# Layer 3 of a four-layer stack: the Walsh-Hadamard transform split between VectorE butterflies and the gate and up weights

## The reference, cut to what matters

```python
def _L3_ffn_ref(input, SU_ug, SU_dp, Wscale_ug, Wscale_dp, W_up, W_gate, W_down):
    HIDDEN = 512
    INTER = 2048
    SCALE = 64.0

    def fwht(x):
        orig_shape = x.shape
        n = orig_shape[-1]
        x = x.reshape(-1, n)
        h = 1
        while h < n:
            x = x.reshape(-1, n // (2 * h), 2, h)
            a, b = (x[:, :, 0, :], x[:, :, 1, :])
            x = jnp.stack([a + b, a - b], axis=2).reshape(-1, n)
            h *= 2
        return (x / jnp.sqrt(jnp.asarray(n, x.dtype))).reshape(orig_shape)
    n = SU_ug.shape[0]
    x = input.reshape(-1, n)
    x = fwht(x * SU_ug) / SCALE
    x_up = x @ W_up.T * (Wscale_ug[:INTER] * SCALE)
    x_gate = x @ W_gate.T * (Wscale_ug[INTER:] * SCALE)
    x = jax.nn.silu(x_gate) * x_up
    x = fwht(x * SU_dp) / SCALE
    x = x @ W_down.T * (Wscale_dp * SCALE)
    return x.reshape(input.shape)
```

## Time and profile before

| | us |
|---|---|
| median of 3 runs | 1707.26 (1704.78 to 1709.21) |
| the profiled execution | 1706.87 |
| its span, first to last instruction | 1705.1 |

### The profile page before, as it was taken

One profiled execution on the slowest core, in us unless ns is written; L12 is line 12 of the kernel. 1 busy time (PEld: TensorE's weight loads), 2 busy tenths in 40 slices (PEclk: granted clock), 3 DMA queues, 4 the chain that ended last, 5 costly groups with the idle time before them and its releaser, 6 DMA issues.

```text
span 1705.1 us, 19577 instructions
## 1 busy us (share of the span) xinstructions
PE 1506.5 (88%) x6453; PEld 970.9 (57%) x6486; DVE 1118.1 (66%) x1718; ACT 969.6 (57%) x1270; POOL 453.4 (27%) x418
## 2 busy tenths in 40 slices
PE   5676579999975899996599999699999999999997
PEld 2222234444432566665544444378788888888886
DVE  6899589999996999995767777754322222222222
ACT  5766499999985889985267868544321221221211
POOL 0000133544421111110144544540231331331311
PEclk9999799999998999998599999899999999999999
DMA  7766642221216877765653545660110110100001
GB/s 279 273 205 208 238 149 64 73 71 62 69 37 178 232 187 182 184 145 206 235 163 136 183 151 170 202 226 1 37 38 1 38 37 1 37 31 8 1 22 77
DMA packets 102998, 206.16 MB, mean 121 GB/s; under 512 B 11061, under 2 KB 27957, under 8 KB 99189
## 3 DMA queue, kind: packets, MB, share of 16 engines
q1 hardware_dynamic: 90308, 173.72, 29.8%
q0 software_dynamic: 12592, 31.20, 8.2%
HBM read 140.13 MB, written 52.17 MB: 113 GB/s over the span
## 4 chain that ended last, share of the span: by engine, by line
PE 49%; DVE 2%; DMA 1%; ACT 1%; issue 0%; POOL 0%; SPq 0%; DVEq 0%; POOLq 0%; ACTq 0%
PE ffn_po L2532 10%; PE ffn_pg L2513 10%; PE ffn_pu L2513 10%; PE moe_psum L1920 8%; PE moe_psum L1941 4%; PE ffn_po L1614 2%; PE ffn_po L1601 2%; PE moe_psum L1859 1%; PE moe_psum L1908 1%; DVE x L2602 1%; PE moe_psum L1931 0%; DMA in_part<-expert_out,moe_source 0%; DVE x L1647 0%; DVE rt_hot_block L2213 0%; DMA rt_consts<-in_route 0%
## 5 line engine op out<-in xcount | busy, mean ns | idle before, releaser
L2435 ACT ACTIVATE up_front<-ffn_pg,ffn_gate_chunk 128x512 f32<-128x512 f32 x64 | 44.1, 689 | 320.7 <-PE ffn_pg L2513 271.7
L2592 DVE SCALAR_TENSOR_TENSOR up_front<-ffn_pu,ffn_up_scale,up_front 128x512 f32<-128x512 f32 x64 | 48.0, 750 | 231.6 <-PE ffn_pu L2513 231.5
L2486 POOL TENSOR_TENSOR ffn_hl<-up_front,ffn_hh 128x512 fp32r<-128x512 f32 x64 | 82.8, 1295 | 396.4 <-ACT ffn_hh L2442 396.4
L2602 DVE SCALAR_TENSOR_TENSOR x<-ffn_po,ffn_out_scale,x 128x512 f32<-128x512 f32 x128 | 87.2, 744 | 146.8 <-PE ffn_po L2532 146.8
L2532 PE MATMUL ffn_po<-ffn_hh,ffn_wh 128*128 128x512 f32 x256 | 100.7, 393 | 4.2 <-DVE x L2602 2.9
L2513 PE MATMUL ffn_pg<-zhi,ffn_wh 128*128 128x512 f32 x256 | 101.5, 396 | 0.5
L2513 PE MATMUL ffn_pu<-zhi,ffn_wh 128*128 128x512 f32 x256 | 100.8, 394 | 0.0
L2513 PE MATMUL ffn_pg<-zhi,ffn_wl 128*128 128x512 f32 x256 | 100.4, 392 | 0.0
L2513 PE MATMUL ffn_pu<-zhi,ffn_wl 128*128 128x512 f32 x256 | 100.4, 392 | 0.0
L2532 PE MATMUL ffn_po<-ffn_hh,ffn_wl 128*128 128x512 f32 x256 | 100.1, 391 | 0.0
L2513 PE MATMUL ffn_pg<-zlo,ffn_wh 128*128 128x512 f32 x256 | 99.6, 389 | 0.0
(11 more groups left out here) (353 smaller groups left out, 4076.5 us busy)
## 6 DMA issues: line engine op xcount, KB each, us to landing
wkv_k<-in_fside SPq DMA_DIRECT2D x64, 256.0 KB, 4.4
ratio<-wkv_fn SPq DMA_DIRECT2D x64, 256.0 KB, 2.4
wkv_ek<-exp_k SPq DMA_DIRECT2D x48, 256.0 KB, 3.0
wkv_ekv<-exp_k_times_v SPq DMA_DIRECT2D x48, 256.0 KB, 3.5
expert_out<-moe_eo SPq DMA_DIRECT2D x39, 256.0 KB, 2.1
up_front<-in_gated SPq DMA_DIRECT2D x8, 1024.0 KB, 5.1
x<-in_x SPq DMA_DIRECT2D x4, 1024.0 KB, 6.8
down_first_a<-in_down_raw SPq DMA_DIRECT2D x16, 256.0 KB, 2.7
```

The lines of the kernel that those rows point to most:

```text
L2435: eng.activation(hf[t], p_g[t][:, :], ACT.Silu, scale=scale).then_inc(*E(f"silu{t}").inc)
L2486: eng.tensor_tensor(hl[t][slot % 2][:, :], hf[t], hh[t][slot % 2][:, :].bitcast(F32), ALU.subtract).then_inc(*E(f"hl{t}").inc)
L2592: eng.scalar_tensor_tensor(hf[t], p_u[t][:, :], scale, hf[t], ALU.mult, ALU.mult).then_inc(*E(f"h{t}").inc)
L2602: last = eng.scalar_tensor_tensor(x[:, o, :], p_o[:, o, :], out_s[:, o:o + 1], x[:, o, :], ALU.mult, ALU.add)
```

## The change

The transform of z is taken apart. Its part over the four channel tiles is done on DVE with butterflies, in float32, before z is split into high and low: `inner` (two pairs, a sum and a difference each) and `outer` (the same across the pairs), eight 128x512 additions or subtractions for each unit. They use the four tiles of z and one spare tile, which is the memory of the first four diagonal matrices. After that z_high and z_low are made once, in the order AS_MADE in which the outer results appear; the second rounding (`round_transformed`, `low_transformed`) is gone, and so is `fwht` with its 32 matmuls for each unit.

The part inside a tile (H128) is symmetric and moves to the weights. `turn_weights(m)` multiplies the gate and up weights of chunk m with H128: 2048 columns in four pieces of 512, two matmuls (high, low) each, into the four banks of gate and up; `high_turned` (ACT) and `low_turned` (DVE) bring each piece back over the old weights as a high and a low part. That is done once for each of the 8 chunks: for the first before the first `cols_of_y`, for the second after down(2), for the others after down(i - 1) at i % 4 = 2 (i = 6, 10, ..., 26). On DVE `low_turned` stands behind `add(i - 1)`. The next step's products wait each for its own piece, so that its bank is free; after i = 3 the first product waits for all four pieces.

The order of the input stage is a new one: gate_up(0) as a whole after cols_of_y(1), then a product of gate, cols_of_y(2), and so on. `gate` of a new unit waits for all of z_low of the unit before, and diagonals(i + 1) stand behind z_low(i) as before.

```diff
+AS_MADE = (2, 0, 3, 1)
...
-        self.minus_H = sb("in3_minus_H", [P, P], F32R)
-        self.diag = [[sb(f"in3_diag{k}_{t}", [P, P]) for t in range(TPB)] for k in range(2)]
+        diag = sb("in3_diag", [P, 2, TPB, P])
+        self.diag = [[diag[:, k, t, :] for t in range(TPB)] for k in range(2)]
+        self.spare = diag[:, 0, :, :].rearrange("p t n -> p (t n)")
...
-    def fwht(self, eng, i):
-        eng.wait_ge(*self.E("minus_H").at(0))
-        eng.wait_ge(*self.E("x").at(CT * i + CT - 1))
-        for k in range(CT):
-            eng.wait_ge(*self.E("z_low").at(CT * i + k))
-            for j in range(CT):
-                h = self.minus_H if (k & j).bit_count() % 2 else self.c["H128"]
-                for t, part in enumerate((self.high(i), self.low(i))):
-                    last = eng.matmul(self.banks[:, j, :], h[:, :], part[:, k, :],
-                                      start=(k + t == 0), stop=(k == CT - 1 and t == 1))
-                if k == CT - 1:
-                    last.then_inc(*self.E("fwht").inc)
...
     def gate(self, eng, n):
         eng.wait_ge(*self.E("x").at(n))
         if n >= CT:
-            eng.wait_ge(*self.E("z_low").at(n - CT))
+            eng.wait_ge(*self.E("z_low").at(n // CT * CT - 1))
         eng.activation(self.g[n % CT][:, :], self.x(n), ACT.Sigmoid).then_inc(*self.E("gate").inc)
 
-    def z_high(self, eng, n):
-        eng.wait_ge(*self.E("z").at(n))
-        eng.activation(self.high(n // CT)[:, n % CT, :], self.g[n % CT][:, :], ACT.Copy).then_inc(*self.E("z_high").inc)
-
-    def gate_and_round(self, eng, i):
-        n = CT * i
-        self.gate(eng, n)
+    def gates(self, eng, i):
         for k in range(CT):
-            if k + 1 < CT:
-                self.gate(eng, n + k + 1)
-            self.z_high(eng, n + k)
-
-    def round_transformed(self, eng, i):
-        for j in range(CT):
-            eng.wait_ge(*self.E("fwht").at(CT * i + j))
-            eng.activation(self.high(i)[:, j, :], self.banks[:, j, :], ACT.Copy).then_inc(*self.E("high").inc)
-
-    def constants(self, eng):
-        eng.tensor_scalar(self.minus_H[:, :], self.c["H128"][:, :].bitcast(F32), -1.0, None, ALU.mult).then_inc(*self.E("minus_H").inc)
+            self.gate(eng, CT * i + k)
+
+    def z_high(self, eng, i):
+        for m, k in enumerate(AS_MADE):
+            eng.wait_ge(*self.E("outer").at(CT * i + m))
+            eng.activation(self.high(i)[:, k, :], self.transformed(k), ACT.Copy).then_inc(*self.E("z_high").inc)
...
+    def inner(self, eng, i, pair):
+        eng.wait_ge(*self.E("z").at(CT * i + 2 * pair + 1))
+        if pair:
+            eng.wait_ge(*self.E("inner").at(CT * i + 1))
+        even, odd = (self.g[2 * pair + k][:, :] for k in range(2))
+        apart = self.g[1] if pair else self.spare
+        eng.tensor_tensor(apart, even, odd, ALU.subtract).then_inc(*self.E("inner").inc)
+        eng.tensor_tensor(even, even, odd, ALU.add).then_inc(*self.E("inner").inc)
+
+    def transformed(self, k):
+        return self.g[(0, 1, 3, 2)[k]][:, :]
+
+    def outer(self, eng, i):
+        eng.wait_ge(*self.E("inner").at(CT * i + CT - 1))
+        g = [t[:, :] for t in self.g]
+        eng.tensor_tensor(g[3], g[0], g[2], ALU.subtract).then_inc(*self.E("outer").inc)
+        eng.tensor_tensor(g[0], g[0], g[2], ALU.add).then_inc(*self.E("outer").inc)
+        eng.wait_ge(*self.E("outer").at(CT * i + 1))
+        eng.tensor_tensor(g[2], self.spare, g[1], ALU.subtract).then_inc(*self.E("outer").inc)
+        eng.tensor_tensor(g[1], self.spare, g[1], ALU.add).then_inc(*self.E("outer").inc)
+
+    def z_low(self, eng, i):
+        for m, k in enumerate(AS_MADE):
+            eng.wait_ge(*self.E("z_high").at(CT * i + m))
+            eng.tensor_tensor(self.low(i)[:, k, :], self.transformed(k), self.high(i)[:, k, :].bitcast(F32),
+                              ALU.subtract).then_inc(*self.E("z_low").inc)
...
-        self.z_low(eng, n)
         self.residual(eng, n + 3)
         self.z(eng, n + 2)
-        self.z_low(eng, n + 1)
+        self.inner(eng, i, 0)
         self.z(eng, n + 3)
-        self.z_low(eng, n + 2)
-        self.z_low(eng, n + 3)
-
-    def low_transformed(self, eng, i):
-        for j in range(CT):
-            eng.wait_ge(*self.E("high").at(CT * i + j))
-            eng.tensor_tensor(self.low(i)[:, j, :], self.banks[:, j, :], self.high(i)[:, j, :].bitcast(F32), ALU.subtract).then_inc(*self.E("low").inc)
+        self.inner(eng, i, 1)
+        self.outer(eng, i)
+        self.z_low(eng, i)
...
+    PIECES = 2 * GU // TIME
+    turned, turned_hi, turned_lo = E("weights_turned"), E("turned_hi"), E("turned_lo")
...
+        p_w = [p_g[0], p_u[0], p_g[1], p_u[1]]
+        piece = lambda t, n: t[:, n * TIME:(n + 1) * TIME]
...
+            def high_turned(m):
+                for n in range(PIECES):
+                    eng.wait_ge(*turned.at(PIECES * m + n))
+                    eng.activation(piece(wh[m % 2], n), p_w[n][:, :], ACT.Copy).then_inc(*turned_hi.inc)
...
+            high_turned(0)
+            inp.gates(eng, 0)
+            inp.z_high(eng, 0)
+            for i in range(1, BATCH):
+                inp.gates(eng, i)
+                for t in range(HT):
+                    silu(i - 1, i - 1, t)
+                inp.z_high(eng, i)
+                for t in range(HT):
+                    high_h(i - 1, i - 1, t)
             high(BATCH, BATCH)
-            for i in range(3, N):
+            for i in range(BATCH - 1, N):
                 for t in range(HT):
                     silu(i, i % U, t)
                 for t in range(HT):
                     high_h(i, i % U, t)
+                if i == BATCH - 1:
+                    high_turned(1)
                 if i % BATCH == 1 and i + 3 < N:
                     high(i + 3, (i + 3) % U)
+                if i % BATCH == 2 and i + 2 < N:
+                    high_turned((i + 2) // BATCH)
...
-                eng.wait_ge(*w_lo.at(i // BATCH))
+                eng.wait_ge(*turned_lo.at(PIECES * (i // BATCH) + PIECES - 1))
+                if i % BATCH == 3 and i >= BATCH and i + 1 < N:
+                    eng.wait_ge(*turned_lo.at(PIECES * (i // BATCH + 1) + p_w.index(ps)))
                 if i >= 1:
                     eng.wait_ge(*E(free).at(i - 1))
                 n = 0
-                for k in range(CT):
+                for m, k in enumerate(AS_MADE):
                     if i < BATCH:
-                        eng.wait_ge(*inp.E("low").at(CT * i + k))
+                        eng.wait_ge(*inp.E("z_low").at(CT * i + m))
...
+            def turn_weights(m, i):
+                eng.wait_ge(*w_lo.at(m))
+                for n in range(PIECES):
+                    if i is not None:
+                        eng.wait_ge(*E(("silu", "h")[n % 2] + str(n // 2)).at(i))
+                    for t, part in enumerate((wh, wl)):
+                        last = eng.matmul(p_w[n][:, :], c["H128"][:, :], piece(part[m % 2], n), start=t == 0, stop=t == 1)
+                    last.then_inc(*turned.inc)
+
             def next_cols(i):
 
-                eng.wait_ge(*inp.E("low").at(CT * i - 1))
+                eng.wait_ge(*inp.E("x").at(CT * i - 1))
                 inp.cols_of_y(eng, i)
 
             before(eng, "zc", "h", "hc", "eo")
+            turn_weights(0, None)
             inp.cols_of_y(eng, 0)
-            inp.fwht(eng, 0)
-            product(0, 0, "gate", 0)
-            product(0, 0, "up", 0)
             next_cols(1)
-            product(0, 0, "gate", 1)
-            product(0, 0, "up", 1)
-            inp.fwht(eng, 1)
+            gate_up(0, 0)
             product(1, 1, "gate", 0)
+            next_cols(2)
             product(1, 1, "up", 0)
-            next_cols(2)
             product(1, 1, "gate", 1)
+            product(1, 1, "up", 1)
             eng.wait_ge(*inp.E("x").at(CT * 2 + CT - 1))
             down(0, 0)
-            product(1, 1, "up", 1)
-            eng.wait_ge(*E("x").at(0))
-            inp.fwht(eng, 2)
             product(2, 2, "gate", 0)
             product(2, 2, "up", 0)
+            eng.wait_ge(*E("x").at(0))
             next_cols(3)
             product(2, 2, "gate", 1)
+            product(2, 2, "up", 1)
             eng.wait_ge(*inp.E("x").at(CT * 3 + CT - 1))
             down(1, 1)
-            product(2, 2, "up", 1)
-            eng.wait_ge(*E("x").at(1))
-            inp.fwht(eng, 3)
             for i in range(3, N + 1):
                 if i < N:
                     gate_up(i, i % U)
-                if i == 3:
-                    eng.wait_ge(*inp.E("low").at(UNITS - 1))
                 down(i - 1, (i - 1) % U)
+                if i == BATCH - 1:
+                    turn_weights(1, i)
+                if i % BATCH == 2 and i >= BATCH and i + 2 < N:
+                    turn_weights((i + 2) // BATCH, i)
...
+            def low_turned(m):
+                for n in range(PIECES):
+                    eng.wait_ge(*turned_hi.at(PIECES * m + n))
```

(85 more changed lines are left out.)

## The result

| | before | after |
|---|---|---|
| median of 6 runs, us | 1708.01 (1701.89 to 1712.70) | 1715.38 (1713.58 to 1722.55) |
| the profiled execution | 1706.87 | 1714.19 |
| its span | 1705.1 | 1712.4 |
| PE's first matmul of layer 3 | 1096.97 | 1094.60 |
| gate_up(4) starts | 1227.21 | 1207.71 |

The ratio of after to before is 1.0049, with a 95% interval of 1.0032 to 1.0067: slower, by some 8 us. The time split at gate_up(4): the stage ahead of it shrank from 130.2 to 113.1 us, the part behind it grew from 477.9 to 504.7.

What follows compares the result with a forecast made beforehand. PE was taken to bound the kernel, busy 1506.5 of 1705.1 us. The sum was 1706.87 - 17.7 (input stage) + 1.7 (clock behind i = 3) + 21.0 (six turns) = 1711.9 us, range 1700 to 1720.

Steps and rivals of the forecast that it cites:

- The start: Turn 0, at half clock, delays cols_of_y(0), which then runs at full rate; unit 0's residual comes 1.2 us later.
- The chain of unit 0: cols_of_y(1) needs diagonals(1), behind z_low(0) on DVE: PE idle 13.3 us, low clock 1.7; unit 0 loses 3 us.
- R: Start of unit 0's residual on DVE, forecast at 1106.2 instead of 1105.00.
- Units 1 to 3: Rest of the input stage: PE works without a break, slack only 0.1 us at diagonals(2); the stage ends 17.7 us sooner.
- The turn at i = 3: Before gate_up(4), which waits for all four pieces: 1.83 us of work, 3.5 idle, then a low clock costing 1.7.
- The six turns: Chunks 2 to 7: the next product starts 3.5 us after down, behind add and piece 0's remainder; +21.0 us in all.
- Rival 1: At the turns matmuls alone count, pieces return in time: 11.0 us instead of 21.0, no gaps, 1696.7 us; chance 0.12.
- Rival 2: The clock falls at each of the six chunk gaps too: 6 x 1.7 us more, 1722.1; chance 0.07.
- Rival 3: POOL's splits of h hold up butterflies or z_low in three units: PE waits 3 x 2.6 us, 1719.7; chance 0.05.
- Rival 4: DVE's list closes a loop with cols_of_y; the input stage saves some 10 us instead of 17.7: 1719.6; chance 0.07.

Runs made afterwards that it cites:

- all three orders: The changed kernel with low_turned ahead of add, diagonals built before in-place butterflies, and cols_of_y(2) right behind gate_up(0): ratio to before 0.9904, median 1693.38 us.

## Why the prediction was right, and where its sizes were off

The forecast was 1711.9, some 5 us slower; measured was 1715.38 with +7.4 between the medians and +9.7 in layer 3. The mechanism was right throughout; several terms were too small. Of the 4.7 us that the sum was short in layer 3, 0.6 is the input stage's, 1.4 the clock's behind i = 3, 1.2 the six turns', and 1.65 the last down's, which the forecast didn't have. That the profiled execution (1714.19) still lies within 2.3 us of the forecast is partly luck: layer 3 began 2.4 us sooner in it than in the kernel before.

- **The start.** Turn 0 ran at the low clock (0.55 in its first 3.5 us) and cols_of_y(0) after it at full rate (1.00 from 1098.1 on), as forecast. The residual of unit 0 began 9.37 us after PE's first matmul (1103.97 less 1094.60); the forecast had 1106.2 less 1096.9, 9.3.
- **The chain of unit 0.** Forecast R + 14.6 for cols_of_y(1) and 13.3 us of idle; measured 1118.75 less 1103.97, 14.8, and 13.47. DVE's rows of after show the butterflies at the 0.60 us that I took:

```profile
1108.63 0.68 DVE L1641 TENSOR_TENSOR in_diag<-up_front 128x512 f32<-128x512 f32 x1
1109.23 0.68 DVE L1642 TENSOR_TENSOR up_front<-up_front 128x512 f32<-128x512 f32 x1
1109.83 0.74 DVE L1633 SCALAR_TENSOR_TENSOR up_front<-up_front,in_su,zhi 128x512 f32<-128x512 f32 x1
```

- **Units 1 to 3.** gate_up(4) came 113.1 us after PE's first matmul against a forecast of 112.6 (1209.5 less 1096.9). -17.7 was -17.1.
- **The turn at i = 3.** The pause was 3.34 where I had 3.5, and the clock fell, as booked. The term that was mis-sized is its price: 3.1 us instead of 1.7. I took the length of the low stretch from rows 7, 3.4 to 3.5 us; here the clock was at 0.50 for all of the first product (5.49 us) and still low at the start of the second (3.10 where 2.75 is usual). With early diagonals the same two took 5.49 and 2.97. In the kernel without later turns the same pause (3.35) cost 1.8: the product behind it took 4.59 and the next 2.75, as this chain shows.

```profile
1211.42 4.59 PE ffn_pg L2510 x12
1216.01 2.75 PE ffn_pu L2510 x12
```

 So 1.7 lay at the lower end of what this cost in three kernels, 1.8 to 3.1, and not in the middle.
- **The six turns.** 3.70 us each instead of 3.5, +22.2 instead of +21.0. The pause was 1.60 (forecast 1.7) and the turn 1.86; what I left out is that the product behind a pause takes 3.00 instead of 2.76 in the chain, even behind one of 0.07 us (low_turned first), and 2.75 behind a turn without any (each piece turned twice). Some 0.08 of it is the first matmul, which is followed by the next after 0.31 us (1263.71 to 1264.02) instead of 0.23; the other 0.16 is that in a stream a matmul starts before the one ahead has ended (recorded with 0.39 us, started every 0.23), which a pause undoes. That could have been read in the chain of the kernel before, where a product behind a transform and 0.12 us of pause takes 3.00 too:

```profile
1137.53 7.46 PE ffn_po L1614 x32
1144.99 0.12 issue
1145.10 3.00 PE ffn_pg L2513 x12
```

- **The end.** The last down waits 2.9 us for add in every kernel here. Behind it the clock fell in after (+1.65) and not in before. Not a part of the change; I come back to it below.
- **The rivals.** Rival 1 (matmuls alone) needed the first remainder within 1.83 us of down. It wasn't so in the changed kernel, but it became nearly true by putting low_turned ahead of add, and that version is indeed faster than before. It was right as a mechanism and named the point from which it decides; it was wrong as a forecast because DVE's list was as it was. Rival 2 (the clock falls at each of the six pauses): behind all six the granted clock stayed at 1.00. The Trainium skill ("TensorE: Matmul & The Clock Gate", section "HAM oscillation") tells of a kernel with waits of some 3 to 5 us between its bursts, each of which began at the low clock. The trace agrees at the one pause of that length, 3.34 us; the six of 1.60 are shorter than those the section speaks of, so the section doesn't speak for this rival. Rival 3 (POOL holds up the butterflies): no butterfly took more than 0.69 us. POOL's first split of h in the input stage (1142.55 to 1145.05) fell where DVE was idle, the next two (from 1163.29 and 1188.10) on add. Rival 4 (the loop over DVE): PE waited for nothing between cols_of_y(1) and the turn in after. It came close: diagonals(2) ended at 1139.50 + 1.65 = 1141.15 and cols_of_y(2) began at 1141.25, the 0.1 us of slack that was forecast; and with an earlier cols_of_y(1) PE waits 1.32 us for z_low(1).

So the question where PE's saving of 15 us went has this answer: the first 17 us are won in the input stage, although PE stands idle there for 13.5; 11 go back as the turns' matmuls at full price, 9.6 as pauses behind an add that nobody was waiting for, 1.4 as slower products behind them and 3.1 as a lowered clock (11 + 9.6 + 1.4 is the 22.2 of above but for rounding). The last down's 1.65 comes on top and isn't the change's.

## What to carry to other kernels

When work is moved to a place where the bounding engine has no slack, its price is not the work alone but the whole way back over the other engines' lists: look what stands in those lists directly ahead of the piece that the bounding engine waits for. An engine that is idle three quarters of the time still holds up another if a task that isn't urgent is ahead of one that is; changing their order cost nothing here and was worth 9.2 us at the six turns and 4.3 at i = 3. A step that leaves an engine's list can leave another step (here the diagonals) at the end of a chain that grew: move it ahead of the chain too, and fill the hole with work that is ready.

## What the runs showed of the hardware

The clock behind one and the same pause isn't the same from one profile to the next. Before the last down PE is idle for 2.9 us in all eight kernels. The last down then took 5.70 to 5.72 us in three of them (before, low_turned first, all three orders) and 7.30 to 7.35 in the other five, at a granted clock of 0.50 in the stretch shown for after. The kernels with all three orders and with the wait for two pieces differ only in how many pieces a chunk's first product waits for, and took 5.72 and 7.30. A pause of 2.9 us thus cost 0 or 1.65 us with the same code around it, one of 3.34 or 3.35 cost 1.8 to 3.1, and in layer 3 none of 1.82 us or less lowered the clock.

What decides it isn't shown; that it also differs between runs of one kernel is likely, since the six runs of after have mean granted clocks from 0.959 in the shortest (span 1711.7) to 0.947 in the longest (1720.7). At the two low stretches of the input stage's start it is the same: from PE's first matmul to unit 0's residual it took 9.26 to 9.58 us in five of the changed kernels (9.37 in after), but 10.70 and 10.73 in the two with low_turned first and without later turns, whose code is the same up to there, and the next low stretch cost those another 0.7. This, with 8.6 us between the earliest and the latest start of layer 3 (1093.0 to 1101.6 in eight profiles), is why small edits here must be read from the stretch that they touch: two spans that differ by 5.7 us can hold the same layer 3 within 0.5.
